# Second block: output projection, row statistics and expert scores in one stage

## The reference, cut to what matters

```python
h = _layernorm(x, axis=-1) * (1 + ca) + sa
x = x + ga * _L1_attn_ref(h, W_Q, W_K, W_V, W_O)      # ends in einsum('dv,bsv->bsd', W_O, heads)
h = _layernorm(x, axis=-1) * (1 + cb) + sb
x = x + gb * _L1_ffn_ref(h, gate_w, w1, w2)
# _L1_ffn_ref begins:
scores = jnp.einsum('ntd,de->nte', h, gate_w)          # 8 experts
probs = jax.nn.softmax(scores, axis=-1)
g, m = jax.lax.top_k(probs of each expert, k)          # each expert takes its best tokens
```

## Time and profile before

| | us |
|---|---|
| time before, median of 3 runs (lowest, highest) | 4417.18 (4415.55, 4419.81) |
| the profiled execution: time, span | 4416.36, 4414.6 |
| PE busy in the span | 3943.4 (89%) |
| DVE busy | 3361.9 (76%) |
| ACT busy | 2537.9 (57%) |
| POOL busy | 1194.1 (27%) |
| mean granted TensorE clock over the span | 0.944 |

### The profile page before, as it was taken

The page is one execution under the profiler, slowest core; times in us unless marked ns, Lnnn a source line. Parts: engine busy times, 40 slices in busy tenths (PEclk is TensorE's granted clock), DMA queues, the critical chain, the costliest instruction groups (busy, mean ns, idle before and its releaser), DMA issues. The chain is left out here.

```text
span 4414.6 us, 98012 instructions
## 1 busy us (share of the span) xinstructions
PE 3943.4 (89%) x39572; PEld 2276.2 (52%) x39572; DVE 3361.9 (76%) x5502; ACT 2537.9 (57%) x3408; POOL 1194.1 (27%) x959
## 2 busy tenths in 40 slices
PE   7999999589989879998966999999999999857996
PEld 4888888346655546665643323232333333444664
DVE  5688888678875478875597899999998987475544
ACT  3566666545544345554323667787888888514553
POOL 1123231377751077761042000000000000132552
PEclk9999999789999989999987999999999999957998
DMA  1011110133320033320044000000000000122444
GB/s 61 12 32 34 36 37 11 32 71 60 61 46 20 7 69 58 64 46 28 0 122 91 14 11 4 11 3 4 10 4 3 11 13 5 48 97 69 90 104 102
DMA packets 311476, 176.70 MB, mean 40 GB/s; under 512 B 221892, under 2 KB 302488, under 8 KB 310424
## 3 DMA queue, kind: packets, MB, share of 16 engines
q1 hardware_dynamic: 279992, 126.60, 13.2%
q0 software_dynamic: 13440, 21.24, 2.7%
q10 hardware_dynamic: 17632, 23.07, 1.6%
HBM read 83.64 MB, written 42.25 MB: 29 GB/s over the span
## 5 line engine op out<-in xcount | busy, mean ns | idle before, releaser
L2187 DVE TENSOR_REDUCE s_tops<-ps 128x2 f32<-128x1024 f32 (+3 forms) x1152 | 1250.2, 1131 | 143.0 <-PE ps L2073 103.6
L2156 ACT ACTIVATE s_weights<-ps 128x1024 f32<-128x1024 f32 (+3 forms) x1152 | 1092.6, 952 | 340.2 <-PE ps L2086 188.3
L2108 PE MATMUL ps<-s_weights,v_flat 128*32 128x256 f32 (+1 forms) x8704 | 690.6, 389 | 7.7 <-ACT s_o_t L2162 6.4
L2067 PE MATMUL ps<-keys,s_q 48*128 48x512 f16 (+3 forms) x2304 | 434.1, 374 | 47.8 <-DVE s_tops L2187 25.9
L2086 PE MATMUL ps<-s_q,keys 50*128 50x512 f16 (+3 forms) x2304 | 433.4, 373 | 46.0 <-DVE s_tops L2187 33.2
L2223 POOL CAST s_shift<-s_minus_top 128x16 f16<-128x16 f32 x32 | 6.3, 196 | 1425.6 <-DVE s_minus_top L2194 1425.6
L582 PE MATMUL ps<-a_qt,a_kt 128*128 128x256 f16 x3072 | 375.3, 273 | 3.8 <-POOL s_ones L537 3.8
L2086 PEld LDWEIGHTS ps<-s_q,keys 50*128 50x128 f16 x2304 | 112.2, 93 | 510.1 <-issue 252.1
L1208 PE MATMUL ps<-attention_w,la_yt 128*128 128x512 f16 x1152 | 288.5, 398 | 57.3 <-DMA la_yt<-la_y_parts 49.8
L1283 ACT ACTIVATE la_weights<-ps 128x1024 f32<-128x1024 f32 x124 | 126.8, 1022 | 347.7 <-PE ps L1198 347.7
L582 PEld LDWEIGHTS ps<-a_qt,a_kt 128*128 128x128 f16 x3072 | 300.9, 98 | 40.3 <-POOL s_ones L537 4.2
(11 more groups left out here) (359 smaller groups left out, 7349.7 us busy)
## 6 DMA issues: line engine op xcount, KB each, us to landing
ex_whole<-in_L_ffn_w_dram ACTq DMA_DIRECT2D x14, 1024.0 KB, 7.1
qk_parts<-a_parts SPq DMA_DIRECT2D x64, 128.0 KB, 3.3
attention_w<-attention_split SPq DMA_DIRECT2D x3, 2048.0 KB, 7.5
keys<-qk_parts SPq DMA_DIRECT2D x48, 128.0 KB, 5.0
s_q<-qk_parts SPq DMA_DIRECT2D x48, 128.0 KB, 4.7
x<-in_x_dram SPq DMA_DIRECT2D x8, 512.0 KB, 9.0
la_table<-in_rotary_dram SPq DMA_DIRECT2D x64, 64.0 KB, 2.0
a_table<-in_rope_dram POOLq DMA_DIRECT2D x8, 512.0 KB, 5.3
```

Of the source, the lines that this page charges most:

```text
L2067: mm = pe.matmul(m.ps[:, bank, 0:width], b.q[rows(half, KEY_PARTS * L1_DH), place % 2, pair, t * P:(t + 1) * P], m.keys[rows(half, KEY_PAR ...
L2108: mm = pe.matmul(m.ps[h * QUAD:(h + 1) * QUAD, OUT, begin:end], m.v_flat[:, first:first + QUAD], weights[:, a % 2, h, begin:end], start=(k ...
L2156: act.activation(weights[:, a % 2, 2 * pair:2 * pair + 2, skip:CHUNK], m.ps[:, bank:end + 1, skip:CHUNK], ACT.Exp).then_inc(s["exp"], 1)
L2187: dve.tensor_reduce(tops[:, u % 2, :, i % 2, t, c], m.ps[:, bank:end + 1, 0:width], AX.X, ALU.max).then_inc(s["max"], 1)
```

## The change

The heads stay in SBUF: `divide_o` writes straight into a tile `heads_out` of 32 tiles, and the stores and the loads back go. The three stages `o1`, `n3` and `es` become one stage `os` (`output_and_scores`), in which each chunk goes the whole way from heads to expert scores. Its order on each engine is written out, without loops in registers:

- PE in turn i: transposes of the heads of chunk i+1, transposes of `h` of chunk i-2, products with `WO` of chunk i, scores of chunk i-2, transposes of the scores of chunk i-3. The scores have the gate's weights stationary (8 columns) and 512 rows moving, so they come out as 8 x 512 and are transposed back.
- DVE in turn i: mean times 1/std of chunk i-1; gate (two instructions of 512 columns), residual sum, statistics and their seven small instructions of chunk i; then scale and shift of `h` of chunk i-1. The residual sum and the shift were POOL's.
- ACT: copies of the transposes, the normalisation (four activations with scale and bias), copies of the scores.
- POOL: only the power, 4 elements wide, once a chunk. SP: the stores of `h`.

The softmax is taken in two parts (chunks 0 to 5, 6 and 7) behind the last chunk. The working tiles lie where the attention's `keys` were, so the names in the rows are `keys`. The first expert's weights are loaded at the start of `ct`, and their low halves are made in the steps 5 to 14 (one piece in 5 to 8, two in 9 to 14).

```diff
 def attention1(nc, m, b):
...
-                def store(u):
...
-                for n in range(2):
-                    sp.wait_ge(o_out[n], 16 * len(UNITS) // 2)
...
-                    if u >= 2:
-                        dve.wait_ge(o_out[u % 2], 16 * (u // 2))
-                    dve.tensor_tensor(o_now[:, u % 2, :, :, :], turned[:, :, :, 0:L1_DH],
+                    heads = m.o[:, j * TPC:(j + 1) * TPC, g * GROUP * L1_DH:(g + 1) * GROUP * L1_DH].rearrange("p t (h d) -> p t h d", h=GROUP)
+                    dve.tensor_tensor(heads, turned[:, :, :, 0:L1_DH],
                                       recip[:, :, :].unsqueeze(3).broadcast_to([P, TPC, GROUP, L1_DH]), ALU.mult).then_inc(s["o_now"], 1)
...
-def attention1_output(nc, m, a):
-def expert_scores(nc, m, b, a):
+def output_and_scores(nc, m, a):
...
+                def turn_h(c):
+                    pe.wait_ge(s["h"], c + 1)
+                    for k in range(KD):
+                        if c:
+                            pe.wait_ge(s["ht"], KD * (c - 1) + k + 1)
+                        for j in range(TPC):
+                            t = pe.transpose(m.ps[:, H_BANK + k, j * P:(j + 1) * P], h[:, c % SLOTS, j, k * P:(k + 1) * P], m.ident[:, :])
+                        t.then_inc(s["h_turned"], 1)
...
+                turn_o(0)
+                pe.wait_ge(s["wo_in"], 16)
+                pe.wait_ge(s["gate_in"], 16)
+                for i in range(CHUNKS + 3):
+                    if exists(i + 1):
+                        turn_o(i + 1)
+                    if exists(i - 2):
+                        turn_h(i - 2)
+                    if exists(i):
+                        products(i)
+                    if exists(i - 2):
+                        scores_of_chunk(i - 2)
+                    if exists(i - 3):
+                        turn_scores(i - 3)
...
+                take_o(0)
+                for i in range(CHUNKS + 3):
+                    if exists(i + 1):
+                        take_o(i + 1)
+                    if exists(i - 1):
+                        normalise(i - 1)
+                    if exists(i - 2):
+                        take_h(i - 2)
+                        take_scores(i - 2)
...
+                def gate(c):
+                    if c >= 2:
+                        dve.wait_ge(s["x"], c - 1)
+                    for half in range(2):
+                        dve.wait_ge(s["out"], 2 * c + half + 1)
...
+                def modulate(c):
+                    now = h[:, c % SLOTS, :, :]
+                    dve.wait_ge(s["normed"], c + 1)
+                    dve.tensor_tensor(now, now, m.modb[:, 4:5, :].broadcast_to([P, TPC, D]), ALU.mult).then_inc(s["scaled"], 1)
+                    dve.wait_ge(s["scaled"], c + 1)
+                    dve.tensor_tensor(now, now, m.modb[:, 3:4, :].broadcast_to([P, TPC, D]), ALU.add).then_inc(s["h"], 1)
...
+                for i in range(CHUNKS + 1):
+                    if exists(i - 1):
+                        minus_mean(i - 1)
+                    if exists(i):
+                        gate(i)
+                        residual(i)
+                        statistics(i)
+                    if exists(i - 1):
+                        modulate(i - 1)
+                for n in range(len(PARTS)):
+                    softmax(n)
...
+                for c in range(CHUNKS):
+                    pool.wait_ge(s["var"], c + 1)
+                    pool.tensor_tensor(m.rstd[:, tiles[c]], m.rstd[:, tiles[c]], m.minus_half[:, tiles[c]], ALU.pow).then_inc(s["rstd"], 1)
...
 def program(nc, a, out):
...
+            m.o = scope.enter_context(nc.sbuf_tensor("heads_out", [P, TILES, D], F32))
             attention1(nc, m, masks)
-        attention1_output(nc, m, a)
...
+            output_and_scores(nc, m, a)
...
-        norm_statistics(nc, m, "n3")
         b = expert_buffers(nc, ctx)
-        expert_scores(nc, m, b, a)
-        choose_tokens(nc, m, b)
+        choose_tokens(nc, m, b, a)
```

More of the change, by code:

```diff
@@ L12 @@
+import math
 from contextlib import ExitStack, contextmanager
@@ new lines, in output_and_scores, with exists @@
+        half_gap = sb("half_gap", [P, TILES])
+        var = sb("var", [P, TILES])
+        minus = sb("minus", [P, TILES])
+        top = sb("top", [P, TILES])
+        total = sb("total", [P, TILES])
+        ot = room(2, KD, CHUNK)
+        gated = room(2, TPC, D)
+        h = room(SLOTS, TPC, D)
+        ht = room(2, KD, CHUNK)
+        scores = room(2, CHUNK)
+        with stage(nc, "os", "wo_in", "gate_in", "o_turned", "ot", "out", "gated", "x", "six", "moments", "var", "rstd", "minus", "normed", "scaled", "h",
+                   "h_out_0", "h_out_1", "h_out_2", "h_turned", "ht", "scores_t", "scores", "turned", "top", "less", "exp", "total", "recip", "probs") as (block, s):
+            h_out = [s[f"h_out_{u}"] for u in range(SLOTS)]
+            tiles = [slice(c * TPC, (c + 1) * TPC) for c in range(CHUNKS)]
+            in_bank = [m.ps[:, bank, 0:TE].rearrange("p (t e) -> p t e", e=EXPERTS) for bank in (PROBS_BANK, O_BANK)]
+            def exists(c):
+                return 0 <= c < CHUNKS
@@ new lines, in scores_of_chunk, with turn_scores @@
+                def scores_of_chunk(c):
+                    pe.wait_ge(s["ht"], KD * (c + 1))
+                    if c:
+                        pe.wait_ge(s["scores"], c)
+                    for k in range(KD):
+                        mm = pe.matmul(m.ps[0:EXPERTS, SCORES_BANK, :], gate_w[:, k, :], ht[:, c % 2, k, :], start=(k == 0), stop=(k == KD - 1))
+                    mm.then_inc(s["scores_t"], 1)
+                def turn_scores(c):
+                    pe.wait_ge(s["scores"], c + 1)
+                    for j in range(TPC):
+                        t = pe.transpose(in_bank[c >= EARLY][:, c * TPC + j, :], scores[0:EXPERTS, c % 2, j * P:(j + 1) * P], m.ident[0:EXPERTS, 0:EXPERTS])
+                    t.then_inc(s["turned"], 1)
@@ L2283, in _, with take_o, normalise @@
-                ahead_in_pairs(act, CHUNKS, load, take)
+                def take_o(c):
+                    if c >= 2:
+                        act.wait_ge(s["out"], 2 * (c - 1))
+                    for k in range(KD):
+                        act.wait_ge(s["o_turned"], KD * c + k + 1)
+                        act.copy(ot[:, c % 2, k, :], m.ps[:, O_BANK + k, :]).then_inc(s["ot"], 1)
+                def normalise(c):
+                    act.wait_ge(s["minus"], c + 1)
+                    if c >= SLOTS:
+                        act.wait_ge(s["h_turned"], KD * (c - SLOTS + 1))
+                        act.wait_ge(h_out[c % SLOTS], 16 * (c // SLOTS))
+                    for j in range(TPC):
+                        t = c * TPC + j
+                        n = act.activation(h[:, c % SLOTS, j, :], m.x[:, t, :], ACT.Identity, bias=minus[:, t:t + 1], scale=m.rstd[:, t:t + 1])
+                    n.then_inc(s["normed"], 1)
@@ new lines, in take_h, with take_scores @@
+                def take_h(c):
+                    if c >= 2:
+                        act.wait_ge(s["scores_t"], c - 1)
+                    for k in range(KD):
+                        act.wait_ge(s["h_turned"], KD * c + k + 1)
+                        act.copy(ht[:, c % 2, k, :], m.ps[:, H_BANK + k, :]).then_inc(s["ht"], 1)
+                def take_scores(c):
+                    act.wait_ge(s["scores_t"], c + 1)
+                    if c >= 2:
+                        act.wait_ge(s["turned"], c - 1)
+                    act.copy(scores[0:EXPERTS, c % 2, :], m.ps[0:EXPERTS, SCORES_BANK, :]).then_inc(s["scores"], 1)
@@ new lines, in _ @@
+                take_o(0)
[7 more added lines that the diff above has]
+                        take_scores(i - 2)
+                for n, part in enumerate(PARTS):
+                    probs = m.probs[:, part.start * TPC:part.stop * TPC, :]
+                    act.wait_ge(s["less"], n + 1)
+                    act.activation(probs, probs, ACT.Exp).then_inc(s["exp"], 1)
@@ L2511, in choose_tokens @@
         found = sb("found", [P, EXPERTS, AREAS])
[L2512 removed]
+        with stage(nc, "ct", "w_in", "w_high", "w_low", "zero", "cleared", "zeroed", "ones", "lanes", "masks", "probs_out", "split", "digit", "trial", "hits", "sum", "count", "kept", "bound",
                    "equal", "rank", "picked", "offset", "dve", "hot", "carried", "gather", "found", "stacked", "chosen") as (block, s):
```

254 lines of the change are left out of this document (93 added, 161 removed).

## The result

The changed kernel takes 4429.6 us (median of 14 runs, 4424.35 to 4436.39), the kernel before 4421.6 us (median of 14 runs, 4414.77 to 4426.28; the three shown above are among them). The ratio is 1.0020 with a 95% interval of 1.0012 to 1.0029, so the change is slower, clear of no change. The medians lie 8.0 us apart, 0.18%, just inside the bound of 0.2% that the prediction drew. The profiled execution of the changed kernel took 4432.82 us, with a span of 4431.2.

What follows compares the result with a forecast made beforehand. The seam was bound by transfers, then PE in `o1` and, at half clock, `es`. New terms sum to 122.1 us against 111.5; with 0.2 in `ct`, 4416.36 + 10.8 = 4427.2, plus 0.8 for the median: 4428.0 us, range 4413 to 4438.

Steps and rivals of the forecast that it cites:

- seam: From the attention's last division to the first DVE instruction of `ct`: 122.1 us where there were 111.5, +10.6.
- turn 1: In `os`, before the engines' waits bind: residual, statistics, power, small product, half a gate and hand-overs, 6.3 us.
- six turns of the ring: The turns of `os` from turn 2 on, with PE's and DVE's passes one behind the other: 82.2 us together.
- behind the last gate, to the last shift's end: Residual, statistics, scale and shift, then chunk 7's small product, normalisation, scale and shift, all exposed: 11.4 us.
- The ring: In `os` PE waits for DVE's `h` and DVE's gate for PE's products: 7.41 + 4.33 = 11.74 us at full clock.
- The turn: One round of PE and DVE in `os`: 11.74 us at full clock, 13.7 us with 4.0 us at half clock.
- The clock: PE's clock falls in each turn of `os`: 4.0 us at half clock, a granted clock between 0.6 and 0.85.
- The rival with the clock held: PE's clock stays at full speed through the turns of `os`: turn 11.74 us, time 4411; chance 0.12.
- The start: In `os`, weights, transposes of chunk 1 and products, to the end of the first gate: 10.7 us.
- The tail: The last chunk's transposes, copies, scores and both softmax parts, at half clock: 9.5 us (6.5 at full clock).
- The power: POOL's power beside DVE's scale and shift doesn't hold DVE up, nothing booked; the rival that it does: 4435, chance 0.07.
- The rival without a ring: PE and DVE overlap in `os`, DVE alone sets a turn at 8.0 us: 34 us less, 4394; chance 0.03.

Runs made afterwards that it cites:

- e1: The changed kernel with TensorE making the products of chunk i ahead of the transposes of `h` of chunk i-2; 4401.9 us.
- e11: The changed kernel with DVE making scale and shift of chunk i-1 ahead of the gate of chunk i, TensorE's order as it was; 4416.0 us.
- e2: The changed kernel plus 8 useless fp32 matmuls of 256 columns per turn where TensorE waits for `h`; 4417.3 us.
- e6: The changed kernel plus a second, useless power of 32 elements on POOL in each turn; 4435.0 us (one run).
- e4: The kernel before with only the heads kept in SBUF, stages, statistics and scores as before; 4422.7 us.
- e5: The changed kernel with scores made rows stationary, straight into the softmax's bank, without the copy and transposes of scores; 4432.3 us.
- e10: A kernel with products first, next heads' transposes later, folded gate and rows-stationary scores, plus useless TensorE work in start and tail; 4388.6 us.
- e7: The changed kernel with the gate multiplied once into the projection's weights, and DVE adding products to `x` straight from PSUM; 4411.8 us.

## Why the prediction was right, and which terms were off

The forecast was 4428.0 us by a ring of waits with a clock that falls in each turn; 4429.6 was measured. Part of that nearness is luck: the forecast stood on a median of three runs (4417.2), and that of 14 is 4421.6; from there the same sum would have given 4432.4. Against the 14 the change costs 8.0 us where I had +10.8. In the profiled seam it costs +9.6 where I had +10.6. The class that I held likelier, slower by over 0.2%, had 0.61; the 8.0 us fall just inside the 8.8 of the other, which had 0.34.

| term | predicted, us | measured, us |
|---|---|---|
| barrier in, start to the end of the first gate | 11.7 | 11.0 |
| turn 1 | 6.3 | 6.1 |
| six turns of the ring | 82.2 | 82.1 |
| behind the last gate, to the last shift's end | 11.4 | 10.6 |
| last chunk's tail | 9.5 | 10.2 |
| barrier out | 1.0 | 1.2 |
| seam | 122.1 | 121.1 |

- **The ring** was read rightly from the two orders, and e1 and e11 show it by cutting it at either engine.
- **The turn**, 13.7 predicted and 13.66 measured, hides two errors that cancel. At full clock it is 11.24, not 11.74 (e2): the seven small instructions of the statistics take 0.69 us with four elements (3882.07 to 3882.76), where I had taken 1.09 from the row with 32. I had called that an upper bound by 0.2; it was too high by 0.4. And the clock costs 2.4 us, not 2.0: in each turn 4.8 us of the ring's TensorE work run at half clock, by that price, where I had booked 4.0.
- **The clock** falls in each turn, as forecast: 0.50 for half of each. What the Trainium skill describes (TensorE: Matmul & The Clock Gate, section on HAM oscillation), that bursts of matmuls with waits between them fall back, agrees with this. The rival with the clock held gave 4411. e2 comes nearest to building it and took 4417.3: it holds the clock in five turns of six, and start and tail kept their price there.
- **The start** was 0.7 shorter. TensorE began at 3835.74, 0.9 us behind the division, then waited for the gate's weights until 3838.72 (1.04 us), which the products don't need.
- **The tail** was 0.7 longer: the transposes of the last `h` stood behind the scores of chunk 6 at half clock (3.58 us), and the softmax's first part behind the last copy of scores.
- **The power** at 1.92 us beside DVE, 1.04 alone, and the shift at 1.23: no lock, as booked; e6 shows it with a power of 6.34 us.
- **In `ct`** four more steps with two pieces cost +0.2: from the first DVE instruction to the one behind the steps it takes 41.50 us (3955.96 to 3997.46) and took 41.28 before (3939.36 to 3980.64). No wait for the weights appeared.
- **The rival without a ring** had 4394 as the time of a kernel with DVE alone in the way. The order kept it from happening here; with the order changed (e1) it is 4401.9.

Where the gain went that the change could have had: keeping the heads in SBUF gives 4.2 us of seam (e4), joining the stages gives 18.1 more when the order is right (107.3 to 89.2), the scores' form gives nothing in the turns (e5), and the order takes 31.9 us back (89.2 to 121.1), some 14.5 of them by the clock. The last figure is an estimate, six turns of 2.42; e2 shows it for five.

## What to carry to other kernels

When stages are joined, write down each engine's order for one turn and follow the waits around: if an engine's order puts work that must wait for its partner ahead of work that the partner waits for, a turn costs the sum of both passes, however idle both look. Try the exchange of the two first; it is two lines. And price a wait on TensorE twice, once as the wait and once as the clock that falls behind it: here useful work moved into the wait gave most (e1, 32 us of seam), filler in the same wait less (e2, 13 us), and filler that ran past the wait gave part of its gain back (e10).

## What was unexpected of the hardware

- The small DVE instructions (four elements a partition) start every 0.08 us when they don't depend on each other, although each shows 0.15 to 0.17 us, and seven of them take 0.69 us; I had scaled them from 32 elements by too little.
- Sixteen fp32 products as the trace counts them, each with a new 128x128 stationary operand and only 8 columns moving, take 1.85 us at full clock, as much as four with 512 columns moving (1.88).
- With waits of 3.5 us in a turn of 13.66 TensorE's clock fell in every turn, with 2.3 us in a turn of about 10 (e7) it held in some and fell in others, and with 0.8 us in a turn of 8.36 (e1) it read 1.00 from 3870 to 3905. The length of the wait alone doesn't decide: in e11 the scores behind a wait of 3.45 us ran at full clock (1.88 us at 3865.12), those behind one of 3.11 us didn't (2.60 us at 3875.81). What decides these runs don't tell.
- A power of 32 elements took 6.34 us beside two wide DVE instructions and 5.46 us alone; the DVE instructions took 1.22 and 1.23 us, as beside a power of four elements.
